# Sixty-four loads of query and key rows issued from the scalar engine's queue in place of the Pool's

## The chip, the cores and the metric

The kernel runs on one core of a Trainium2 chip. A core has a matrix engine (PE, TensorE), a vector engine (DVE), a scalar engine (ACT), a Pool engine (GpSimd) and a sync engine (SP); all of them run their own instruction streams and meet only at semaphores. SP, ACT and Pool can also issue DMA transfers, and the core's 16 DMA engines carry them out. The metric is the device time of one execution in microseconds (us); lower is better.

## The reference, cut to what matters

The layer takes x of shape [2, 1024, 256] in float32. It normalises x and adds two branches to it: causal attention with 16 heads of 16 features and an ALiBi bias, and a mixture of experts (16 experts, the two best for each token, and one shared expert).

```python
xn = _layernorm(x, axis=-1)
x = x + _L0_attn_ref(xn, qkv_w, ...) + _L0_ffn_ref(xn, gate_w, ...)

# attention
qkv = hidden_states @ qkv_w.T + qkv_b
scores = jnp.einsum('bqhd,bkhd->bhqk', q, k) * scale
scores = jnp.where(causal[None, None], scores + bias[None], NEG)
out = jnp.einsum('bhqk,bkhd->bqhd', softmax(scores), v) @ out_w.T + out_b

# experts
_, selected = jax.lax.top_k(sigmoid(x @ gate_w) + expert_bias, 2)
shared = _silu(x @ shared_gate_w) * (x @ shared_up_w) @ shared_down_w
for e in range(16):
    routed += comb[:, e:e+1] * (_silu(x @ gate_e) * (x @ up_e) @ down_e)
```

## The kernel before, in words

The work goes in stages, in this order on every engine.

1. **Projections and routing.** PE forms queries, keys, values and router scores. The queries and keys are cut into three bfloat16 parts each, and SP stores them in DRAM (`qk_parts`, 16 stores, L432). The bias rows of the attention go to DRAM too (`aux_rows`). The router gives every token two slots in a list sorted by expert, and Pool scatters the normalised tokens into it by 32 indirect transfers (`sorted_tokens`, L542).
2. **Shared expert.** Four chunks of 512 tokens. ACT takes one tanh of each (L676), and semaphore `s_g1` tells that PE has made a chunk.
3. **Expert tiles.** The sorted list is 48 tiles of 128 slots. SP loads a tile (`x_in`, L443); PE transposes it (L1137); ACT copies it from PSUM to SBUF (`hx`, L681 for the first three, L691 from then on); PE multiplies it by its expert's weights (L1147); ACT takes a tanh (L686); DVE makes the product (L925, L928); PE multiplies again (L1163); DVE copies the result (L935) and SP stores it (L447). Every tile passes through ACT twice, so nothing of this stage goes on while ACT is elsewhere. Beside the tiles, PE and DVE find the row maxima of attention group 0 (L1176, L942), 32 pieces over the 48 tiles.
4. **Attention.** Eight groups (one sequence, four heads each). Four buffers hold the rows of a group: `qs`/`ks` for groups 0 and 1 (and 4 and 5), `qk` for groups 2 and 3 (and 6 and 7). At its start Pool begins to gather the expert outputs (`yg`, L575). The attention ends with the output projection (L1268).

The helper `load(queue, side, g, half)` fills one half of one side (0 is queries, 1 is keys) of a group's buffer by four transfers: three from `qk_parts` of 3, 2 and 1 parts (L375; 48, 32 and 16 partitions) and one from `aux_rows` (L377; 12 or 15 partitions). It takes the issuing queue as its first argument. A group is four such calls, 16 transfers; groups 0 to 3 are 64 transfers, 16 calls. Below, a call is one set of four transfers. Groups 4 to 7 are another 64, which SP issues during the attention, each group when the buffer it takes is free.

Before, Pool issues groups 0 to 3 behind the scatter. It waits for the shared expert's outputs (`s_sh`), the stores of `aux_rows` and `qk_parts` (`s_auxst`, `s_parts`) and the landed scatter (`s_scat`), the last because group 3's buffer lies where `xn` lay, which the scatter reads. The first use of these loads is the first piece of group 0's maxima, behind expert tile 0 on PE (L1176). Groups 1 to 3 are first used in the attention.

A DMA has a semaphore count that it adds when it lands. Issuing one occupies the issuing engine's stream, and what is behind it in that stream waits.

Of the kernel before, what the change touches and what calls it, by code (L numbers as in the profile page):

```python
# [19 lines left out]
TT = T // P  # L20
KC = D // P
HG = 4
E, F, K_TOP = 16, 128, 2
# [35 lines left out]
NBUF = 4  # L59
RING = 6  # L60
# [79 lines left out]
def build(nc, x, qkv_w, qkv_b, out_w, out_b, slopes, gate_w, ebias, sg_w, su_w, sd_w, e_gu, e_dn,  # L140
          c_ident, c_perm, c_bf, c_pos, c_coef, c_sel, c_row, y):
    ctx = ExitStack()
    with ctx:
# [3 lines left out]
        def sem(name):  # L147
            return ctx.enter_context(nc.semaphore(name))
# [99 lines left out]
        def bank(n, w=CH, m=P):  # L248
            return ps[0:m, n * CH:n * CH + w]
# [33 lines left out]
        s_free = sem("bank_freed")  # L283
        s_res = sem("parts_ready")
        s_mid = sem("mid_ready")
        s_parts = [sem(f"parts_stored{i}") for i in range(RING)]
# [4 lines left out]
        s_auxst = sem("aux_stored")  # L291
# [5 lines left out]
        s_scat = sem("tokens_sorted")  # L297
# [4 lines left out]
        s_sh = sem("shared_out_ready")  # L302
# [49 lines left out]
        NJ, NQK = len(JOBS), len(QKJ)  # L352
# [4 lines left out]
        DMA = 16  # L357
# [5 lines left out]
        def load(queue, side, g, half):  # L363

            dst, order = (q_buf, k_buf)[side][g % NBUF], (Q_PARTS, K_PARTS)[side]
            done = (s_first, s_ld)[g // NBUF][half][g % NBUF]
            cols = slice(half * CH, (half + 1) * CH)
            for t0, n in ((0, 3), (3, 2), (5, 1)):
                p0 = order[t0]
                if side == 0:  # L370
                    src = qkd[0, p0:p0 + 1, g:g + 1, :, :, cols].rearrange("n g d j s -> (g n) d j s")
                    src = src.broadcast_to([n, HD, HG, CH])
                else:
                    src = qkd[1, 0:n, g:g + 1, :, :, cols].rearrange("n g d j s -> (g n) d j s")
                queue.dma_start(dst[HD * t0:HD * (t0 + n), :, cols], src).then_inc(done, DMA)  # L375
            rows = (N_ALIBI, N_AUX)[side]
            queue.dma_start(dst[AUX0:AUX0 + rows, :, cols],  # L377
                         auxd[side, g:g + 1, :, 0:rows, cols].rearrange("g j r s -> r (g j) s")
                         ).then_inc(done, DMA)

        @block.sync
        def _(sp):
# [44 lines left out]
            for i in range(NQK):  # L427
                _, fc, tc = JOBS[QKJ[i]]
                side, g0 = fc // 2, tc // 2 * 4 + fc % 2 * 2
                cols = slice(tc % 2 * CH, (tc % 2 + 1) * CH)  # L430
                sp.wait_ge(s_res, i + 1)
                sp.dma_start(qkd[side, :, g0:g0 + 2, :, :, cols].rearrange("n g d j s -> (g d j) n s"),  # L432
                             parts[:, i % RING, :, :]).then_inc(s_parts[i % RING], DMA)
# [64 lines left out]
        def _(pool):  # L498
# [34 lines left out]
            for n in range(4):  # L533
                side, half = n // 2, n % 2
# [17 lines left out]
            copy_v(0, 0)  # L552
            copy_v(1, 1)

            pool.wait_ge(s_sh, TT // 2)
            pool.wait_ge(s_auxst, 4 * DMA)
            for i, stored in enumerate(s_parts):
                pool.wait_ge(stored, DMA * len(range(i, NQK, RING)))
            pool.wait_ge(s_scat, K_TOP * TT * DMA)
            for g in range(NBUF):  # L560
                for half in range(2):
                    for side in range(2):
                        load(pool, side, g, half)

            for u in range(4):
                pool.wait_ge(s_ys[u], NT // 4 * DMA)
            pool.wait_ge(s_sha, TT // 2)
# [44 lines left out]
        def _(act):  # L612
# [59 lines left out]
            for c in range(4):  # L672
                act.wait_ge(s_g1, c + 1)
                if c >= 2:
                    act.wait_ge(s_h, c - 1)
                sc.activation(th[:, c % 2, :], bank(2 * c), ACT.Tanh, scale=0.5).then_inc(s_th, 1)  # L676

            def evacuate_tokens(k):

                act.wait_ge(s_hxt, k + 1)  # L680
                sc.activation(hx[:, (k + 1) % 2, 1:, :], bank((k + 1) % 2)[:, P:(1 + KC) * P].rearrange(  # L681
                    "p (c n) -> p c n", n=P), ACT.Copy).then_inc(s_hx, 1)
# [645 lines left out]
```

## Time and profile before

| what | us |
|---|---|
| median of 3 runs | 526.53 (524.24 to 529.89) |
| the profiled execution's own time | 525.04 |
| its span, first to last instruction | 523.2 |
| PE busy | 461.9 (88%) |
| DVE busy | 324.3 (62%) |
| ACT busy | 249.4 (48%) |
| POOL busy | 198.4 (38%) |

The profile is of one execution. A wait is charged to the operation that came last. The chain of waits is followed back from the last instruction, at each step to what released it. A queue (SPq, POOLq) is the part of an engine that issues; its rows give the time in which it was issuing a transfer, not the time in which the transfer moved data. For Pool the issuing counts as busy time too; for SP and ACT it doesn't.

### The profile page before, as it was taken

How to read it: one execution, taken by the hardware profiler on the slowest of the kernel's cores; microseconds unless marked ns; L12 is line 12 of the kernel's file. 1: busy time of each engine (PE TensorE's matmuls, PEld its weight loads, DVE VectorE, ACT ScalarE, POOL GpSimd, SP SyncE). 2: the span in 40 equal slices, each digit the busy share in tenths (PEclk: the TensorE clock that was granted, in tenths of full speed). 3: DMA queues.
4: the chain of work that ended last, by engine and by line, in shares of the span. 5: the costliest groups of instructions: out<-in, count | busy, mean ns of one | idle time of the engine just before them, and what ended most of it. 6: DMA issues, size and time to landing. Idle time of an engine off the chain costs nothing.

```text
span 523.2 us, 9031 instructions
## 1 busy us (share of the span) xinstructions
PE 461.9 (88%) x3049; PEld 271.6 (52%) x3050; DVE 324.3 (62%) x610; ACT 249.4 (48%) x567; POOL 198.4 (38%) x239
## 2 busy tenths in 40 slices
PE   4595999737859999995999999999999999999998
PEld 4454788525635666763445354444444444332676
DVE  3869985413425656676867877778586867744232
ACT  2620652112213333332767676676676757678300
POOL 3470777699940000006888888800000000000000
PEclk9799799977779999997999999999999999999999
DMA  9898999799999434424113333221120000010022
GB/s 282 188 403 256 318 323 291 246 170 144 188 174 203 127 110 121 130 79 140 42 49 104 108 86 106 71 76 61 48 82 18 3 3 3 1 13 6 3 89 73
DMA packets 65705, 64.60 MB, mean 123 GB/s; under 512 B 21935, under 2 KB 59539, under 8 KB 65635
## 3 DMA queue, kind: packets, MB, share of 16 engines
q1 hardware_dynamic: 51506, 47.85, 30.9%
q0 software_dynamic: 13056, 15.83, 15.0%
q8 instruction: 24, 0.39, 0.3%
q10 hardware_dynamic: 1104, 0.41, 0.3%
q14 instruction: 15, 0.11, 0.1%
HBM read 37.27 MB, written 27.13 MB: 123 GB/s over the span
## 4 chain that ended last, share of the span: by engine, by line
PE 66%; DVE 13%; DMA 12%; issue 2%; ACT 2%; POOL 2%; SPq 1%; POOLq 0%; DVEq 0%
PE ps L1248 12%; PE ps L1222 10%; PE ps L1234 10%; PE ps L1147 7%; PE ps L1268 5%; DMA x_in<-sorted_tokens 5%; DVE mx L970 5%; PE ps L1043 4%; PE ps L1163 4%; DMA ks<-aux_rows 2%; PE ps L1237 2%; PE ps L1223 2%; PE ps L1137 2%; ACT pt L718 2%; DMA x_sb<-x 1%
## 5 line engine op out<-in xcount | busy, mean ns | idle before, releaser
L718 ACT ACTIVATE pt<-ps 128x512 f32<-128x512 f32 (+3 forms) x384 | 167.1, 494 | 79.7 <-PE ps L1237 55.2
L970 DVE TENSOR_REDUCE mx<-ps 128x1 f32<-128x384 f32 (+6 forms) x189 | 153.3, 863 | 52.4 <-PE ps L1223 51.1
L1248 PE MATMUL ps<-pt,vg 128*32 128x512 f32 (+3 forms) x768 | 71.9, 492 | 0.0
L575 POOL DMA_INDIRECT yg<-sorted_outputs,slot_i x32 | 32.0, 1000 | 94.2 <-DMA sorted_outputs<-y_out 85.4
L1147 PE MATMUL ps<-w_gu,hx 128*128 x192 | 58.3, 432 | 3.8 <-issue 2.2
L1234 PE MATMUL ps<-qs,ks 111*128 111x512 bf16 (+3 forms) x192 | 55.7, 331 | 3.7 <-DMA qs<-nr 3.0
L1234 PE MATMUL ps<-qk 111*128 111x512 bf16 (+3 forms) x192 | 54.9, 329 | 1.8 <-ACT pt L718 0.3
L935 DVE COPY y_out<-ps 128x256 f32<-128x256 f32 x48 | 20.4, 425 | 56.4 <-PE ps L1163 52.7
L1237 PE MATMUL ps<-cbf 128*128 128x128 bf16 x256 | 52.4, 221 | 0.0
L691 ACT ACTIVATE hx<-ps 128x384 f32<-128x384 f32 (+1 forms) x48 | 22.9, 477 | 61.3 <-PE ps L1137 58.6
L1222 PE MATMUL ps<-qk 108*128 108x512 bf16 (+3 forms) x192 | 50.2, 328 | 1.8 <-DVE mx L970 1.3
L1223 PE MATMUL ps<-cbf 128*128 128x128 bf16 x224 | 46.9, 222 | 0.0
L1147 PEld LDWEIGHTS ps<-w_gu,hx 128*128 128x128 f32 x192 | 36.1, 208 | 13.2 <-issue 8.3
L542 POOL DMA_INDIRECT sorted_tokens<-xn,slot_i x32 | 32.8, 1024 | 25.0 <-DVE slot_i L877 15.6
L1222 PE MATMUL ps<-ks,qs 108*128 108x512 bf16 (+3 forms) x144 | 38.5, 335 | 2.4 <-DVE mx L970 1.2
L547 POOL COPY vg<-v_sb 128x512 f32<-128x512 f32 x8 | 4.8, 614 | 89.6 <-PE ps L1248 89.6
L1248 PEld LDWEIGHTS ps<-pt,vg 128*32 128x32 f32 x768 | 19.6, 109 | 33.8 <-issue 20.8
L1163 PE MATMUL ps<-w_dn,hx 128*128 x96 | 33.6, 433 | 1.2 <-ACT hx L691 0.9
L590 POOL TENSOR_SCALAR yg<-yg,gates 128x256 f32<-128x256 f32 x32 | 30.2, 944 | 1.2
L1137 PE MATMUL ps<-ident,x_in 128*128 128x128 f32 x96 | 20.0, 292 | 12.0 <-DMA x_in<-sorted_tokens 11.9
L1234 PEld LDWEIGHTS ps<-qk 111*128 111x128 bf16 x192 | 17.7, 98 | 23.9 <-ACT pt L718 8.4
L686 ACT ACTIVATE te_h<-ps 128x128 f32<-128x128 f32 x48 | 13.3, 277 | 34.5 <-PE ps L1147 34.5
(175 smaller groups left out, 737.9 us busy)
## 6 DMA issues: line engine op xcount, KB each, us to landing
sorted_tokens<-y_out SPq DMA_DIRECT2D x12, 512.0 KB, 5.0
qk_parts<-parts SPq DMA_DIRECT2D x16, 384.0 KB, 3.5
x_in<-sorted_tokens SPq DMA_DIRECT2D x48, 128.0 KB, 2.7
sorted_outputs<-y_out SPq DMA_DIRECT2D x48, 128.0 KB, 1.7
w_gu<-e_gu SPq DMA_DIRECT2D x1, 2816.0 KB, 12.9
x_sb<-x SPq DMA_DIRECT2D x4, 512.0 KB, 8.4
w_dn<-e_dn SPq DMA_DIRECT2D x1, 2048.0 KB, 8.7
y<-x_sb SPq DMA_DIRECT2D x16, 128.0 KB, 1.7
```

The lines of the kernel that those rows point to most:

```text
L542: g_.indirect_dma_start(out=xsd, out_offset=bass.IndirectOffsetOnAxis(ap=slot_i[:, k, t:t + 1], axis=0), in_=xn[:, t, :], in_offset=None). ...
L575: g_.indirect_dma_start(out=yg[:, n % 4, :], out_offset=None, in_=ysd, in_offset=bass.IndirectOffsetOnAxis(ap=slot_i[:, k, t:t + 1], axis= ...
L718: sc.activation(pt[:, s % 4, j, lo:CH], bank(n % 3)[:, lo:CH], ACT.Exp).then_inc(s_exp, 1)
L970: last = v.reduce_max(dst, src, axis=AX.X)
L1137: ins = te.transpose(ps[:, v * CH + (1 + c) * P:v * CH + (2 + c) * P], x_in[:, u, c * P:(c + 1) * P], ident[:, :])
L1147: ins = te.matmul(bank(2 + w, 2 * F), hx[:, 1 - w, 1 + c, :], w_gu[:, bass.ds(e, 1), c, :].rearrange("p o f -> p (o f)"), start=c == 0, st ...
L1163: te.matmul(bank(4 + w, D), hx[:, w, 0, :], w_dn[:, bass.ds(e, 1), :].rearrange("p o f -> p (o f)"), start=True, stop=True).then_inc(s_dn, 1)
L1222: te.matmul(ps[:, at + c:at + e], q, k_buf[g % NBUF][0:K_MAX, j, c:e], start=True, stop=e < w)
L1223: ins = te.matmul(ps[:, at + w - P:at + w], idb, mask_q, start=False, stop=True)
L1234: ins = te.matmul(out[:, lo:CH], k_buf[g % NBUF][0:K_EXP, j, kb * P:(kb + 1) * P], q_buf[g % NBUF][0:K_EXP, j, qc * CH + lo:(qc + 1) * CH] ...
L1237: ins = te.matmul(out[:, lo:lo + P], idb, mask_k, start=False, stop=True)
L1248: ins = te.matmul(ps[32 * j:32 * j + 32, OUT_BANK * CH + lo:(OUT_BANK + 1) * CH], vg[:, par, kb, j, :], pt[:, s % 4, j, lo:CH], start=kb = ...
```

## The change

The wait block and the 16 calls of `load` for groups 0 to 3 leave Pool's stream. ACT's stream gets them, between the fourth tanh of the shared expert and the first copy of an expert tile. ACT waits for `s_free` at its last count (the projections are out of PSUM), `s_auxst` and `s_parts` before the first call, and for `s_scat` only before group 3. The wait on the shared expert's outputs is gone; ACT's own four tanhs already waited for the four `s_g1` counts.

```diff
@@ gpsimd
             copy_v(0, 0)
             copy_v(1, 1)
 
-            pool.wait_ge(s_sh, TT // 2)
-            pool.wait_ge(s_auxst, 4 * DMA)
-            for i, stored in enumerate(s_parts):
-                pool.wait_ge(stored, DMA * len(range(i, NQK, RING)))
-            pool.wait_ge(s_scat, K_TOP * TT * DMA)
-            for g in range(NBUF):
-                for half in range(2):
-                    for side in range(2):
-                        load(pool, side, g, half)
-
             for u in range(4):
                 pool.wait_ge(s_ys[u], NT // 4 * DMA)
             pool.wait_ge(s_sha, TT // 2)
@@ scalar
                 sc.activation(th[:, c % 2, :], bank(2 * c), ACT.Tanh, scale=0.5).then_inc(s_th, 1)
+
+            act.wait_ge(s_free, NJ)
+            act.wait_ge(s_auxst, 4 * DMA)
+            for i, stored in enumerate(s_parts):
+                act.wait_ge(stored, DMA * len(range(i, NQK, RING)))
+            for g in range(NBUF):
+                if g == NBUF - 1:
+                    act.wait_ge(s_scat, K_TOP * TT * DMA)
+                for half in range(2):
+                    for side in range(2):
+                        load(act, side, g, half)
 
             def evacuate_tokens(k):
```

ACT's stream before, from the last tanhs of the shared expert to the first copies of expert tiles (`th` is the shared expert's tanh, `hx` a transposed tile, `te_h` a tile's tanh):

```order
L676 ACTIVATE th<-ps 128x512 [waits shared_h_ready,shared_hidden_ready] x2
L681 ACTIVATE hx<-ps 128x256 [waits tile_transposed] x2
L686 ACTIVATE te_h<-ps 128x128 [waits tile_gate_up_ready] x2
L681 ACTIVATE hx<-ps 128x256 [waits tile_transposed]
L702 UNCONDITIONAL_BRANCH
```

The same place in the changed kernel (its lines from there on are numbered differently):

```order
L666 ACTIVATE th<-ps 128x512 [waits shared_h_ready,shared_hidden_ready] x2
L375 DMA qs<-qk_parts 48x4x512 [waits parts_stored2,parts_stored3,parts_stored1,parts_stored4,parts_stored0,parts_stored5,aux_stored,bank_freed]
L375 DMA qs<-qk_parts 32x4x512
L375 DMA qs<-qk_parts 16x4x512
L377 DMA qs<-aux_rows 12x4x512
L375 DMA ks<-qk_parts 48x4x512
...
L377 DMA qk<-aux_rows 15x4x512
L682 ACTIVATE hx<-ps 128x256 [waits tile_transposed] x2
L687 ACTIVATE te_h<-ps 128x128 [waits tile_gate_up_ready] x2
```

All 64 transfers now stand ahead of the first tile's copy in the same stream.

Pool's stream in the changed kernel, from the scatter to the gather of expert outputs:

```order
L542 DMA sorted_tokens<-xn,slot_i 6144x256 x31
L547 COPY vg<-v_sb 128x32x16 [waits bank_freed]
L547 COPY vg<-v_sb 128x32x16
L565 DMA yg<-sorted_outputs,slot_i 128x256 [waits tile_out_stored3,tile_out_stored2,shared_added,tile_out_stored1,tile_out_stored0]
```

Pool has nothing between its two copies of values and the gather, which waits for all tile outputs as before. SP's stream is the same in both kernels.

## Rows read from the trace of the kernel before

**Rows 1.** The page: busy time by engine, and the chain of waits.
```profile
PE 461.9 (88%) x3049; PEld 271.6 (52%) x3050; DVE 324.3 (62%) x610; ACT 249.4 (48%) x567; POOL 198.4 (38%) x239
...
PE 66%; DVE 13%; DMA 12%; issue 2%; ACT 2%; POOL 2%; SPq 1%; POOLq 0%; DVEq 0%
```

**Rows 2.** Chain of waits, 70 to 160 us: start us, us, what.
```profile
93.02 5.44 DMA sorted_tokens<-xn,slot_i
...
105.11 11.95 DMA ks<-aux_rows
...
118.34 12.69 DMA x_in<-sorted_tokens
...
138.94 15.02 DMA x_in<-sorted_tokens
```

**Rows 3.** Timeline of ACT: start us, duration us, line, operation [idle before].
```profile
94.31 0.60 ACT L676 ACTIVATE th<-ps 128x512 f32<-128x512 f32 x1 [3.91 <-PE ps L1043]
101.03 0.87 ACT L681 ACTIVATE hx<-ps 128x256 f32<-128x256 f32 x2 [6.12 <-PE ps L1137]
...
107.47 0.49 ACT L691 ACTIVATE hx<-ps 128x384 f32<-128x384 f32 x1 [0.64 <-PE ps L1137]
...
158.39 0.49 ACT L691 ACTIVATE hx<-ps 128x384 f32<-128x384 f32 x1 [1.27 <-PE ps L1137]
...
186.45 0.49 ACT L691 ACTIVATE hx<-ps 128x384 f32<-128x384 f32 x1 [1.10 <-PE ps L1137]
...
212.94 0.49 ACT L691 ACTIVATE hx<-ps 128x384 f32<-128x384 f32 x1 [1.13 <-PE ps L1137]
...
233.93 0.28 ACT L691 ACTIVATE hx<-ps 128x128 f32<-128x128 f32 x1 [0.98 <-PE ps L1155]
```

**Rows 4.** Timeline of Pool's queue: its first calls of load and its last.
```profile
99.22 2.75 POOL L375 DMA_DIRECT2D qs<-qk_parts  x3 [4.07 <-DMA sorted_tokens<-xn,slot_i]
101.97 0.56 POOL L377 DMA_DIRECT2D qs<-aux_rows  x1
102.52 2.60 POOL L375 DMA_DIRECT2D ks<-qk_parts  x3
105.11 0.56 POOL L377 DMA_DIRECT2D ks<-aux_rows  x1
...
152.19 0.56 POOL L377 DMA_DIRECT2D qk<-aux_rows  x1
```

**Rows 5.** Waits of PE, 95 to 240 us: total us, times, longest.
```profile
PE ps L1137 <- DMA x_in<-sorted_tokens: 11.9, 5, 3.6
PE ps L1176 <- DMA ks<-aux_rows: 7.9, 1, 7.9
```

**Rows 6.** Timeline of SP's queue: the 16 transfers of group 5, then of group 7.
```profile
306.25 2.46 SPq L375 DMA_DIRECT2D qs<-qk_parts  x3
308.76 0.55 SPq L377 DMA_DIRECT2D qs<-aux_rows  x1
309.35 7.29 SPq L375 DMA_DIRECT2D ks<-qk_parts  x3
...
330.84 0.59 SPq L377 DMA_DIRECT2D ks<-aux_rows  x1
...
369.40 2.27 SPq L375 DMA_DIRECT2D qk<-qk_parts  x3
371.72 0.66 SPq L377 DMA_DIRECT2D qk<-aux_rows  x1
372.42 6.25 SPq L375 DMA_DIRECT2D qk<-qk_parts  x3
378.72 0.59 SPq L377 DMA_DIRECT2D qk<-aux_rows  x1
379.35 5.30 SPq L375 DMA_DIRECT2D qk<-qk_parts  x3
384.69 0.55 SPq L377 DMA_DIRECT2D qk<-aux_rows  x1
385.29 5.26 SPq L375 DMA_DIRECT2D qk<-qk_parts  x3
390.59 0.59 SPq L377 DMA_DIRECT2D qk<-aux_rows  x1
```

**Rows 7.** Source views of L375, L377, L432, L443: issue ns min/median/max; landing.
```profile
L375 SPq DMA_DIRECT2D ks<-qk_parts x12: 737/2806/3348, 277.8 to 327.6; - x12
...
DMA to landing us min/median/max: 5.9/14.1/20.5
...
L432 SPq DMA_DIRECT2D qk_parts<-parts x16: 359/360/366, 55.6 to 81.4; - x16
...
L443 SPq DMA_DIRECT2D x_in<-sorted_tokens x48: 328/345/1242, 98.5 to 221.5; - x48
```

**Rows 8.** Stretches: busy us of PE, PEld, DVE, ACT, POOL; clock, DMA share, GB/s.
```profile
101.00:154.70 53.70, 33.56 (x131) 23.47 (x131) 15.41 (x44) 10.08 (x27) 48.58 (x63) 0.77 1.06 166
...
186.50:213.00 26.50, 26.03 (x130) 17.88 (x131) 16.25 (x46) 9.22 (x25) 0.00 (x0) 1.00 0.39 119
...
379.00:391.00 12.00, 11.76 (x83) 4.75 (x81) 9.97 (x12) 9.21 (x20) 0.00 (x0) 1.00 0.24 77
```

**Rows 9.** Timeline of PE: four matmuls of one tile at low and at full clock.
```profile
117.94 1.99 PE L1147 MATMUL ps<-w_gu,hx 128*128 x4
...
189.24 1.13 PE L1147 MATMUL ps<-w_gu,hx 128*128 x4
```

## The prediction

> **What bounds the kernel now.** I read the page first. PE is busy for 88% of the span and holds 66% of the chain of waits; DMA holds 12% of it and Pool 2% [rows 1]. A share over the whole span doesn't say what a change between 95 and 235 us is worth, so I went to the chain of that stretch. There it isn't PE that sets the end. The chain runs through the scatter's landing, then 11.95 us for a load of group 0's bias rows, then two loads of an expert tile that took 12.69 and 15.02 us [rows 2]. A tile's load usually needs far less. The reader is to see that the loads of groups 0 to 3 stand in the way of the tiles: PE waits 7.9 us for the first of them and 11.9 us for tiles [rows 5].
>
> The timeline of ACT gives the size of that loss, since ACT copies each tile once. Tile 0 is copied at 107.47, tile 12 at 158.39, tile 24 at 186.45 and tile 36 at 212.94 [rows 3]. Between the last two, with Pool silent and the clock at its full level [rows 8], 12 tiles take 26.5 us, 2.21 a tile. The first 12 took 50.9, which is 24.4 more, and the next 12 took 28.1, which is 1.6 more. So at most some **26 us** can be won here, and only if nothing new stands in the way.
>
> **What the change removes.** Pool's queue issued for 53.5 us, from 99.22 to 152.75 [rows 4]. Pool's next work is the gather, which waits for all tile outputs, so its free time is worth nothing. What counts is the 26 us of slow tiles: they vanish if the loads are over before the tiles start. I price this at -26.0.
>
> **What it adds.** ACT ends its fourth tanh at 94.9 and before now copied its first tile at 101.03 [rows 3]. Now 64 transfers stand between these two. The waits ahead of them cost little: the scatter began its last piece at 93.02 and landed 5.44 us later [rows 2], long before group 3 is reached, and the stores of `qk_parts` were issued by 81.8 at the latest [rows 7]. The price is in the issuing.
>
> The trace of before doesn't show ACT issuing these loads, but it shows SP issuing 64 of the same shapes and sizes for groups 4 to 7. The timeline of SP's queue is the view that decides the case. Group 7 takes 21.8 us to issue, from 369.40 to 391.18: its four calls take 3.0, 6.9, 5.9 and 5.9 us [rows 6]. The first call goes out into an empty queue; from the second on, a transfer can be issued only at the pace at which earlier ones move. One large load of keys holds SP for 2.8 us at the median, and the least such hold was 0.74 us [rows 7]. A contiguous load of a tile holds it for 0.35 us and a store of `qk_parts` for 0.36 us [rows 7], so it isn't the number of bytes alone. The share of the 16 DMA engines in use during group 7 was only 0.24 [rows 8]: the queue is full while most of the DMA engines idle.
>
> The Trainium skill has a reason for this. Its page "DMA: Bandwidth & Descriptors", section "Why a DMA increments its semaphore by 16 and not by 1", says that a DMA is split over the largest number of engines, up to 16, that divides the outermost size of both sides, and that on SP's and ACT's queues these are always the lowest-numbered ones, whereas Pool's rotate. By it the loads with 3 and 2 parts outermost would run on three and two engines; the share of 0.24, which is 3.8 of 16, agrees.
>
> ACT issues 16 calls with no pause between groups, so it meets the empty queue once: 3.0 + 6.9 + 14 x 5.9 = 92.5, rounded to **93 us** of issuing. ACT is free at 94.9 + 93 = 188 instead of 101, which puts every tile 87 us later. I take group 7's pace and not group 5's, whose last three calls took 7.36 us each (309.35 to 331.43) [rows 6]: Pool was gathering beside group 5, and nothing moves beside ACT's loads after the first ten microseconds, since tile work stands still.
>
> Ends for this term: below, the pace at which Pool's transfers moved. The last was issued at 152.19 and landed at most 20.5 us later [rows 4, 7], so 16 calls took up to 73.5 us, 4.6 each, and ACT would be free at 168. Above, group 5's pace: 3.1 + 15 x 7.36 = 113.5, and ACT is free at 208.
>
> **A smaller term.** PE will have idled for some 85 us before the tiles. Behind an idle stretch four matmuls of a tile took 1.99 us against 1.13 at full clock [rows 9], the two levels being 1.2 and 2.4 GHz. I add 2 us for two or three tiles at the low level. Between 0 (the slow first 12 tiles that I removed held this already, and my 26.5 for them doesn't) and 6 us (every tile of the first six a microsecond late) is possible. The loads themselves then wait for nobody: group 0 has landed long before its maxima.
>
> **Sum.** 87 - 26 + 2 = +63 us on the last tile, which before was copied at 233.93 [rows 3]. The attention behind it is unchanged, instruction by instruction, and waits for the tiles (maxima of group 0, then the negated maxima), so all of it moves with them. The profiled execution took 525.04 us, 1.84 more than its span; 525.0 + 63 = 588. The median of the runs is 1.5 above that execution, so I forecast **589.5 us**. The likeliest case's own range is 580 to 608.
>
> **The rivals.**
>
> *Faster: issuing costs what SP's other transfers cost.* If ACT could issue without being held, at 0.36 us each [rows 7], 64 would take 23 us, ACT would be free at 118 and the tiles start 17 us late. Most of the 26 us would come back, because group 0 lands early: 17 - 26 + 2 = -7, so 519.5 us. It decides at 0.47 us a transfer, 30 us in all. The Trainium skill's same page, section "Issuing engines are not separate DMA queues", speaks for it: the time to initiate a DMA "is usually small relative to the DMA itself". The trace speaks against it, with 2.8 us for one, and no call of this kind took under 3.0 us even on an empty queue. Chance 0.03 for faster, and 0.02 for ending within 1%.
>
> *ACT's queue holds more than SP's.* If none of ACT's transfers were held, each call would cost what SP's first does, 3.0 us: 16 x 3.0 = 48, free at 143, +42 - 26 + 2 = +18, so 544.5 us. For it speaks only that ACT's queue is nearly unused in this kernel. Against it: SP is held after four or five transfers, so ACT's would have to be some tens deeper. Chance 0.04.
>
> *Pool's pace.* The transfers move at 4.6 us a call as they did from Pool: free at 168, +67 - 26 + 2 = +43, so 569.5 us. SP's rows speak against it, since they show 5.9 with more than three quarters of the DMA engines idle, where Pool's ran beside tile traffic with the share at 1.06 [rows 8]. Chance 0.06.
>
> *The change doesn't do what it says.* The order of ACT's stream shows that it does: no tile's copy stands ahead of a load.
>
> **How the numbers follow.** The likeliest case has 0.85. Range **575 to 608**: it reaches from half-way between Pool's pace and SP's quiet pace up to group 5's pace, and leaves out the first two rivals, most of the third and a slice of the main one. I count a difference under 1% (5 us) as no change, about what a measurement of this kernel can tell. Slower by over 1%: 0.85 + 0.04 + 0.06 = 0.95; within 1%: 0.02; faster: 0.03.
>
> **What would show it.** In the timeline of ACT's queue, L375 and L377 should stand from about 95 to 188 us, each call near 6 us from the third on, with a DMA share near 0.2 to 0.3 once the first 10 us are over. Between some 102 and 188 us PE, DVE and Pool should have no work. ACT's first copy of a tile should be at about 188, the last near 297 (233.93 + 63), and 12 tiles in the first third should take some 27 to 29 us in place of 50.9. The attention should last as long as before. I'd be wrong if the calls took under 4.5 us each or if ACT's tile copies came between them; and the 26 us would be wrong if the first tiles were slow again without the loads beside them.

## The result and the profile after

| | before | changed |
|---|---|---|
| median, us | 525.38 (523.81 to 529.89, 4 runs) | 589.82 (589.38 to 590.48, 4 runs) |
| profiled execution, us | 525.04 | 589.38 |
| its span, us | 523.2 | 587.6 |
| PE busy, us | 461.9 | 453.8 |
| POOL busy, us | 198.4 | 148.0 |

The ratio is 1.1212 (95% interval 1.1138 to 1.1285): the kernel became 64 us slower. The forecast was 589.5 us in a range of 575 to 608.

The page of the changed kernel, busy time and the chain of waits, answers [rows 1]:

```profile
PE 453.8 (77%) x3049; PEld 267.3 (45%) x3050; DVE 323.8 (55%) x610; ACT 249.3 (42%) x567; POOL 148.0 (25%) x175
...
PE 65%; ACTq 16%; DVE 11%; DMA 3%; issue 2%; ACT 2%; SPq 1%; DVEq 0%
```

ACT's queue, which held no part of the chain before, now holds 16% of it, some 94 us. DMA fell from 12% to 3%. ACT's busy time is what it was, since this profile doesn't count issuing in it: whoever reads only busy shares sees an engine at 42% and misses the cause.

Timeline of ACT in the changed kernel, start and duration in us (ACTq is its queue). It answers [rows 3] and has calls as in [rows 6]:

```profile
95.06 0.60 ACT L666 ACTIVATE th<-ps 128x512 f32<-128x512 f32 x1 [3.91 <-PE ps L1044]
95.35 3.69 ACTq L375 DMA_DIRECT2D qs<-qk_parts  x3
99.08 0.58 ACTq L377 DMA_DIRECT2D qs<-aux_rows  x1
99.69 7.61 ACTq L375 DMA_DIRECT2D ks<-qk_parts  x3
107.34 0.60 ACTq L377 DMA_DIRECT2D ks<-aux_rows  x1
107.97 6.15 ACTq L375 DMA_DIRECT2D qs<-qk_parts  x3
...
187.18 5.51 ACTq L375 DMA_DIRECT2D qk<-qk_parts  x3
192.73 0.60 ACTq L377 DMA_DIRECT2D qk<-aux_rows  x1
193.38 0.66 ACT L682 ACTIVATE hx<-ps 128x256 f32<-128x256 f32 x2 [97.72 <-issue]
...
200.04 0.49 ACT L692 ACTIVATE hx<-ps 128x384 f32<-128x384 f32 x1 [0.64 <-PE ps L1138]
...
224.05 0.49 ACT L692 ACTIVATE hx<-ps 128x384 f32<-128x384 f32 x1 [1.14 <-PE ps L1138]
...
250.41 0.49 ACT L692 ACTIVATE hx<-ps 128x384 f32<-128x384 f32 x1 [1.10 <-PE ps L1138]
...
276.83 0.49 ACT L692 ACTIVATE hx<-ps 128x384 f32<-128x384 f32 x1 [1.14 <-PE ps L1138]
...
297.78 0.28 ACT L692 ACTIVATE hx<-ps 128x128 f32<-128x128 f32 x1 [0.98 <-PE ps L1156]
```

The issuing fills 95.35 to 193.33, the whole gap before the first tile's copy. A word on how tiles are counted here and in the prediction: the copy called tile n is the L692 (before: L691) copy of step n of ACT's tile loop. It moves the product of tile n and, up to step 44, the transposed tokens of tile n + 3, which is why it stands some 6.5 us behind the first copy of all; with the tanh, every tile passes through ACT three times. The differences between steps don't depend on the name. The first 12 tiles, steps 0 to 12, now take 24.0 us (200.04 to 224.05) where they took 50.9. Stretches of the changed kernel (us; busy PE, PEld, DVE, ACT, POOL; granted clock, DMA share, GB/s), as [rows 8]:

```profile
107.00:193.00 86.00, 0.00 (x0) 0.00 (x0) 0.00 (x0) 0.00 (x0) 0.00 (x0) 0.50 0.25 77
193.00:200.00 7.00, 4.66 (x13) 3.30 (x13) 1.15 (x4) 1.60 (x5) 0.00 (x0) 0.59 0.17 50
200.00:224.00 24.00, 23.79 (x130) 17.66 (x130) 14.93 (x43) 9.21 (x24) 0.00 (x0) 1.00 0.42 127
```

For 86 us no compute engine does anything, and even then the DMA share is only 0.25, at 77 GB/s. That is the row to learn from: nothing is busy, and yet the queue doesn't go faster. What PE waited for, 90 to 300 us (total, times, longest), against [rows 5]:

```profile
PE ps L1148 <- ACT hx L682: 88.1, 1, 88.1
...
PE ps L1138 <- DMA x_in<-sorted_tokens: 6.3, 1, 6.3
```

The five waits for tiles have become one, the wait for `ks` is gone, and a single wait for ACT replaced them.

### The profile page after: what moved, and what is told of

It reads as the page before. It is cut to its first block, busy times and chain, and to the rows that moved or that the text cites. A ratio compares the mean times of both kernels' runs of the same rounds, so it can differ in the third digit from the quotient of the medians.

```text
span 587.6 us, 9031 instructions
## 1 busy us (share of the span) xinstructions
PE 453.8 (77%) x3049; PEld 267.3 (45%) x3050; DVE 323.8 (55%) x610; ACT 249.3 (42%) x567; POOL 148.0 (25%) x175
## 4 chain that ended last, share of the span: by engine, by line
PE 65%; ACTq 16%; DVE 11%; DMA 3%; issue 2%; ACT 2%; SPq 1%; DVEq 0%
ACTq L375 15%; PE ps L1249 11%; PE ps L1223 9%; PE ps L1235 9%; PE ps L1148 8%; PE ps L1044 6%; PE ps L1269 5%; DVE mx L971 5%; PE ps L1164 4%; PE ps L1238 2%; PE ps L1224 2%; PE ps L1138 2%; ACTq L377 2%; DMA x_sb<-x 1%; PE ps L1177 1%
## 5 line engine op out<-in xcount | busy, mean ns | idle before, releaser
L1148 PE MATMUL ps<-w_gu,hx 128*128 x192 | 54.4, 408 | 89.2 <-ACT hx L682 88.1
L1148 PEld LDWEIGHTS ps<-w_gu,hx 128*128 128x128 f32 x192 | 33.7, 195 | 97.1 <-issue 92.2
L926 DVE SCALAR_TENSOR_TENSOR te_h<-te_h,ps 128x128 f32<-128x128 f32 x48 | 13.3, 278 | 97.7 <-ACT te_h L687 97.7
L692 ACT ACTIVATE hx<-ps 128x384 f32<-128x384 f32 (+1 forms) x48 | 22.9, 477 | 38.8 <-PE ps L1138 36.1
L1164 PE MATMUL ps<-w_dn,hx 128*128 x96 | 32.4, 419 | 1.2 <-ACT hx L692 0.9
L1269 PE MATMUL ps<-wo_t,ot 128*128 128x256 f32 x128 | 28.3, 381 | 1.3 <-DVE ot L1032 1.3
```

The source lines that it names most:

```text
L1148: ins = te.matmul(bank(2 + w, 2 * F), hx[:, 1 - w, 1 + c, :], w_gu[:, bass.ds(e, 1), c, :].rearrange("p o f -> p (o f)"), start=c == 0, st ...
L1164: te.matmul(bank(4 + w, D), hx[:, w, 0, :], w_dn[:, bass.ds(e, 1), :].rearrange("p o f -> p (o f)"), start=True, stop=True).then_inc(s_dn, 1)
L1269: ins = te.matmul(bank(4 + m % 4, D), ot[:, n // QT * 4 + hg, n % QT * P:(n % QT + 1) * P], wo_t[:, hg, :], start=hg == 0, stop=hg == 3)
```

## The experiments

Two theories stood at the start. **Few engines:** a load whose outermost size is 3 or 2 is moved by that many DMA engines, the queue fills, and the issuing engine is held at their pace. **Cost of issuing:** the hold comes with the transfer's bytes, rows or number, or with ACT's queue as such. Ratios below are to the kernel before on the same chip. In the three kernels with "flat" in their names the loads of groups 0 to 3 read other rows than the attention needs, so they show what a load costs and are no kernels to use.

| kernel | median us | ratio, 95% interval |
|---|---|---|
| the changed kernel | 589.82 | 1.121, 1.114 to 1.129 |
| e_act16 | 561.85 | 1.073, 1.068 to 1.078 |
| e_flat48 | 532.17 | 1.013, 1.010 to 1.017 |
| e_half | 570.63 | 1.087, 1.082 to 1.093 |
| e_half_late | 543.77 | 1.036, 1.033 to 1.040 |
| e_pool16 | 500.25 | 0.953, 0.947 to 0.958 |
| e_all16 | 500.37 | 0.953, 0.950 to 0.956 |
| e_paced | 514.54 | 0.980, 0.975 to 0.985 |
| e_pool_flat48 | 514.48 | 0.982, 0.974 to 0.989 |
| e_flat_paced | 522.10 | 0.953, 0.946 to 0.960 |
| e_16_paced | 523.55 | 0.957, 0.948 to 0.965 |

The last two ran on a chip on which the kernel before took 547.32 us; only their ratios compare with the others.

### Loads of one part each, from ACT (e_act16)

```diff
-            for t0, n in ((0, 3), (3, 2), (5, 1)):
+            for t0, n in (... if g >= NBUF else [(t, 1) for t in range(6)]):
...
+                    p0 = order[t0]
-                    src = qkd[1, 0:n, ...]
+                    src = qkd[1, p0:p0 + n, ...]
```

> ACT issues as in the changed kernel, but each load of 3, 2 or 1 parts is cut into loads of one part (16 partitions outermost on both sides): 7 transfers a call in place of 4, 112 in all, same bytes. Theory (a load with 3 or 2 parts outermost runs on so few DMA engines that the queue fills and ACT is held): no hold is left, each transfer costs its bare issue of about 0.6 us, 16 x 7 x 0.6 = 67 us in place of 98, ACT free at about 162 and the time near 558 us (552 to 567). Rival (issuing costs per byte or per row whatever the shape, or the ACT queue is slow in itself): ACT is held for 98 us or longer, with 48 more transfers, so 590 to 617 us.

561.85 us, inside the theory's 552 to 567. Timeline of ACT's queue, third call:

```profile
103.84 3.80 ACTq L377 DMA_DIRECT2D qs<-qk_parts  x6
107.67 0.56 ACTq L379 DMA_DIRECT2D qs<-aux_rows  x1
```

A call went from 6.1 to 4.4 us although it has seven transfers and not four. Each takes 0.63 us (3.80 / 6), from the first call to the last, and ACT was free at 166.0. More transfers of the same rows and bytes cost less time, so the hold wasn't the price of a transfer, of a byte or of ACT's queue as such.

### The same 64 transfers with another outermost size (e_flat48)

```diff
+                if g < NBUF:
+                    src = qkd[side, 0, g:g + n, :, :, cols].rearrange("g d j s -> (g d) j s")
                 queue.dma_start(dst[HD * t0:HD * (t0 + n), :, cols], src).then_inc(done, DMA)
```

> The changed kernel with the same 64 transfers from ACT, of the same sizes and the same 48, 32 and 16 partitions, but the L375 loads of groups 0 to 3 read 48, 32 or 16 neighbouring rows of DRAM, so that the outermost size is 48, 32 or 16 on both sides and not 3, 2 or 1 on the source's. (The rows are not those that the group needs: the scores of groups 0 to 3 are of other values.) Theory (the outermost size decides how many DMA engines move a load, and so how long ACT is held): no hold, 64 x 0.6 = 38 us plus a little at the start, ACT free at about 135 and the time near 530 us (526 to 538). Rival (ACT is held by the bytes or rows of a transfer, or by a queue that is full at a fixed number of transfers): ACT is held for about 98 us again, 585 to 592.

532.17 us. This is the cleanest of the tests, since number, bytes and partitions are those of the change. What it changes beside the outermost size is which rows are read: other ones, and each once, where a load of queries read one part two or three times. e_act16 covers that, since it read the rows of the change and wasn't held either. ACT's queue, the third call and the first copy of a tile; then the stretch of the loads:

```profile
101.69 1.89 ACTq L377 DMA_DIRECT2D qs<-qk_parts  x3
103.62 0.56 ACTq L379 DMA_DIRECT2D qs<-aux_rows  x1
...
136.96 0.66 ACT L684 ACTIVATE hx<-ps 128x256 f32<-128x256 f32 x2 [40.38 <-issue]
```

```profile
98.00:136.00 38.00, 3.34 (x12) 2.01 (x12) 3.60 (x7) 0.00 (x0) 0.00 (x0) 0.58 1.11 213
```

A call took 2.5 us, not 6.1, and the DMA share rose from 0.25 to 1.11. With e_act16 beside it, the bytes, the rows and the number of transfers are ruled out as the cause of the hold: the outermost size is. Behind this measurement stands the Trainium skill, "DMA: Bandwidth & Descriptors", section "Why a DMA increments its semaphore by 16 and not by 1", by whose rule the loads ran on 3 or 2 engines and now on 16. Which engines moved a load isn't in these rows; the share agrees with the number.

The packets of ACT's queue come closer to it (packets, MB, share of 16 engines; the changed kernel at 107 to 193 us, then this one at 98 to 136):

```profile
q10 hardware_dynamic: 6652, 6.32, 23.7%
```

```profile
q10 hardware_dynamic: 7419, 6.67, 95.2%
```

Counted from the same records, two or three packets of ACT's queue were in flight for 73% of the 86 us, and 13 or more for 3%; in this run 13 or more were in flight for 80% of the time. A packet of the changed kernel took 49 ns on average (0.237 x 16 x 86 us / 6652), nearly all of them moving 1 KB. An estimate from that: if three engines share the load of 192 KB and two the load of 128 KB, each moves 64 KB of either, and an engine that is in both moves 128 packets a call, 6.3 us; a call took 6.1.

And 532 is still slower than before: 40 us of bare issuing on ACT put the first copy of a tile 35.9 us later (136.96 against 101.03), more than the 29 us that quiet tiles give back.

### Half of the calls from ACT (e_half, e_half_late)

Against the changed kernel, and condensed:

```diff
-            for g in range(NBUF):
+            for g in range(2):
                 ... load(act, side, g, half)
+            for g in range(2, NBUF):        # in Pool's stream, behind the scatter
+                ... load(pool, side, g, half)
```

> ACT issues groups 0 and 1 only (32 transfers, 8 calls), Pool issues groups 2 and 3 behind the scatter as before. Theory (every microsecond of issuing on ACT moves the tiles by as much): the eighth call ended at 145.0 in the changed kernel, 48 us earlier than the sixteenth, so about 541 us, up to 550 where Pool's transfers slow ACT's. Rival (the price is one fixed thing, such as tiles waiting for the last group to land, not the number of calls): 575 us or more.

570.63 us: the theory's 541 to 550 was missed by 20 us and more, and the rival's 575 wasn't reached. ACT's queue showed why:

```profile
96.16 3.67 ACTq L375 DMA_DIRECT2D qs<-qk_parts  x3
99.87 0.58 ACTq L377 DMA_DIRECT2D qs<-aux_rows  x1
100.48 18.42 ACTq L375 DMA_DIRECT2D ks<-qk_parts  x3
```

Pool issued its own loads of the same shape from 101.58 to 131.36. ACT's second to fourth calls took 19, 17 and 13 us, and the last four, without Pool's, 5.9 to 6.4. Stretches with Pool's loads and without them:

```profile
101.00:131.00 30.00, 1.35 (x4) 0.58 (x4) 0.50 (x1) 0.00 (x0) 24.91 (x32) 0.55 0.95 146
150.00:174.00 24.00, 0.00 (x0) 0.00 (x0) 0.00 (x0) 0.00 (x0) 0.00 (x0) 0.50 0.23 74
```

Together the two queues and the rest moved 146 GB/s. ACT was free at 174.6. I had allowed 9 us for Pool's neighbourhood and it cost 30. So the next run kept Pool away:

```diff
+                        pool.wait_ge(s_yo, 4 + 4 * (4 * (g - 2) + 2 * half + side))
                         load(pool, side, g, half)
```

> ACT issues groups 0 and 1; Pool issues groups 2 and 3, but each of its 8 calls waits until 4, 8, 12 ... 32 tiles are out, so that none runs beside ACT's. Theory (the 29 us by which e_half missed came from Pool's transfers slowing ACT's; alone, ACT's price goes by the number of calls): the eighth call ends near 145 us, the tiles start 48 us earlier than in the changed kernel, and Pool's calls beside the tiles cost 0 to 6 us: 541 to 548 us. Rival (half the calls cost more than half for another reason): 560 or more.

543.77 us.

```profile
144.62 0.66 ACT L691 ACTIVATE hx<-ps 128x256 f32<-128x256 f32 x2 [49.94 <-issue]
```

ACT was free at 144.6, 48.8 us earlier than in the changed kernel, and the time fell by 46.1. The price of the change therefore goes by the calls that ACT issues. And Pool's loads slowed ACT's more than the bytes tell: the 146 GB/s of e_half are well under the 239 of e_pool16 below. Whether ACT's loads slowed Pool's as much isn't shown by these rows.

### Pool again, with even loads (e_pool16, e_all16)

These are the kernel before with the edit of e_act16, for groups 0 to 3 and for all eight.

> The kernel before, Pool issuing, with the loads of groups 0 to 3 cut into one part each (7 transfers a call). If Pool's transfers slow the tiles by uneven use of the DMA engines, as the queue of SP and ACT does, the first 12 tiles take under 40 us in place of 50.9 and the time falls to 510 to 518. If it is the bytes alone that stand before the tile loads, no change: 520 to 530; Pool's issuing lengthens from 50 to about 61 us.

500.25 us, 24 us faster than before and 10 us below the 510 to 518 expected. Stretch of 110 to 140 us, in e_pool16 and then in the kernel before:

```profile
110.00:140.00 30.00, 29.58 (x147) 21.49 (x148) 17.33 (x48) 10.68 (x28) 30.00 (x60) 0.94 0.90 239
```

```profile
110.00:140.00 30.00, 19.19 (x78) 14.51 (x78) 8.27 (x25) 5.37 (x14) 30.00 (x39) 0.72 1.07 170
```

PE is busy for 29.6 of 30 us where it was for 19.2, and DMA moved 239 GB/s at a lower share. The loads of groups 2 and 3 landed sooner too (KB each, median us from issue to landing, first in the kernel before, then in e_pool16):

```profile
qk<-qk_parts POOLq DMA_DIRECT2D x8, 192.0 KB, 16.5
```

```profile
qk<-qk_parts POOLq DMA_DIRECT2D x48, 64.0 KB, 3.2
```

The first 12 tiles took 25.8 us. So the slow tiles came from the way these loads are cut: the kernel before paid for it through the tiles' loads, the changed kernel through ACT's stream. Two things differ here, though, the outermost size and the size of a transfer (at most 64 KB in place of 192); the last runs take them apart.

> The kernel before, Pool issuing groups 0 to 3, with all eight groups' loads cut into one part each (SP's for groups 4 to 7 too). The theory says that SP is held less (28 transfers x 0.6 = 17 us a group in place of 22 to 25). SP's hold was not on the path, so the same time as with Pool's loads cut alone, 498 to 502 us; a gain of up to 3 us if the negated maxima waited behind the loads, a loss if more transfers crowd the queue.

500.37 us, the same. SP was held less (group 7 took 18.4 us in place of 22.5 in e_pool16), and nobody had waited for that hold.

### Is it the shape alone? (e_paced, e_pool_flat48, e_flat_paced, e_16_paced)

```diff
 # e_paced: behind group 0, one call for three tiles; for two tiles in e_flat_paced and e_16_paced
+                        if g:
+                            pool.wait_ge(s_yo, PACE0 + PACE * (4 * (g - 1) + 2 * half + side))
                         load(pool, side, g, half)
```

> The kernel before, Pool issuing, with group 0 at once and each of the other 12 calls held until 4, 7, 10 ... 37 tiles are out (a wait of Pool on the count of copied tile outputs). Theory (the 26 us of slow tiles come from loads that crowd the tile loads): only group 0's four calls crowd them, about half of the loss returns, 508 to 517 us. Rival (the loss is the clock or the first tiles' own): 522 to 530.

514.54 us: 10 us of the 26 came back, with every load cut as it was before, so at least that part of the slow tiles was due to the loads beside them, and not to the clock or the first tiles as such. The first 12 tiles took 36.5 us; PE waited 7.8 us for group 0's loads among them. Each of the next two dozens took 28.1 and 28.3 us in place of 26.4, so even one confined call for three tiles costs something.

> The kernel before, Pool issuing its 64 transfers, but the L375 loads of groups 0 to 3 read 48, 32 or 16 neighbouring rows, so that the outermost size is 48, 32 or 16 on both sides. (Other rows than the group needs: the scores of groups 0 to 3 are of other values.) Theory (the slow tiles of before come from loads that run on 3 or 2 DMA engines, not from the number of transfers or their bytes): the first 12 tiles take 25 to 28 us and the time is 498 to 505 us. Rival (cutting the loads helped because each was smaller, or because 112 transfers leave gaps for the tiles' loads): 518 to 527 us.

514.48 us: neither theory's number. The outermost sizes were even (48, 32 and 16), yet the first 12 tiles took 39.8 us. The chain of waits, 90 to 160 us:

```profile
117.05 10.27 DMA x_in<-sorted_tokens
127.36 0.45 PE ps L1139 x2
127.98 15.90 DMA x_in<-sorted_tokens
```

```profile
110.00:140.00 30.00, 22.87 (x98) 15.90 (x97) 11.35 (x33) 6.92 (x18) 26.70 (x49) 0.87 1.06 239
```

Pool issued a call in 2.2 us (e_pool16: 3.6), 35 us in all, with a share of 1.06 and tile loads of 10 and 16 us on the chain. My reading was that Pool put its bytes before the tiles' loads faster than DMA could move both, so that even loads aren't enough and their pace counts too. The size of a transfer was the other explanation, so:

> Pool's 64 transfers from 48, 32 and 16 neighbouring rows again (other values for groups 0 to 3), but after group 0 each of the other 12 calls waits until 1, 3, 5 ... 23 tiles are out, one call for two tiles (about 4.4 us) where the run before issued one in 2.2 us with the share of the DMA engines at 1.06. Theory (with the loads spread over the engines, what slowed the tiles there was the pace at which Pool put bytes before them): the slow stretch shrinks to group 0's, the first 12 tiles take 26 to 30 us and the time is 499 to 505 us. Rival (the tiles wait because each of Pool's transfers is large, up to 192 KB, whatever the pace): 510 to 516.

A ratio of 0.953, by estimate 500 us on a chip like the first ones (0.953 x 525), with the transfers as large as before.

```profile
131.88 0.49 ACT L696 ACTIVATE hx<-ps 128x384 f32<-128x384 f32 x1 [0.64 <-PE ps L1142]
...
156.34 0.49 ACT L696 ACTIVATE hx<-ps 128x384 f32<-128x384 f32 x1 [1.14 <-PE ps L1142]
```

The first 12 tiles took 24.5 us. Size by itself is ruled out; pace it was. Group 0's four calls weren't paced here nor in e_paced, yet the first 12 tiles took 24.5 us here and 36.5 there, beside confined loads that were paced more slowly. What remains open is that this run and the next were on another chip than the runs they are set against.

> The kernel before with the loads of groups 0 to 3 cut into one part each and the 12 calls behind group 0 held until 1, 3, 5 ... 23 tiles are out. With even loads at Pool's own pace of 3.6 us a call the tiles already ran at their undisturbed rate, so nothing is left to win: 498 to 503 us. If the remaining waits for tiles (2.9 us) go, 1 to 2 us less.

A ratio of 0.957, by the same estimate 502 us, with 27.4 us for the first 12 tiles: nothing was left to win beyond e_pool16.

## Why the prediction was right, point by point

- **ACT is held by the issuing: right, 5 us too small.** 93 us forecast, 98.0 measured. The steady call was 5.9 and came out at 6.1 (14 calls from 107.97 to 193.36). The first two were 3.0 and 6.9 and came out at 4.3 and 8.3: the late expert weights and the first tiles' loads were still moving (159 GB/s from 98 to 107 us against 77 afterwards), a likely cause that no run took apart. These two make 2.7 us of the excess, and the 0.2 us on each of the other 14 the rest. I had said that nothing moves beside ACT's loads after ten microseconds and then priced those ten as if they were quiet too. The first copy of a tile came 92.4 us late instead of 87.
- **Slow tiles go away: right, 2.6 us too small.** The first 12 tiles gave back 26.9 us (50.9 to 24.0) and the next 12 gave 1.7: 28.6 in place of 26, and 24.0 lies below the 27 to 29 that I had named as the sign. My undisturbed rate, 2.21 us a tile, was that of tiles 24 to 36. The undisturbed first 12 run at 2.00 here, and the last 11 at 1.9 in both kernels. In PE's and DVE's code the first and the last 12 tiles are written out and the two dozen between are a hardware loop; that this is the reason was not tested, and the last three copies are also smaller.
- **A slow start of PE: not seen.** I had added 2 us and 0.2 came. The clock stood at 0.50 of full in the 86 idle microseconds and at 0.59 in 193 to 200, but the start from the first copy to tile 0 took 6.66 us against 6.44 before, and from 200 on the clock was full. The kernel before started its tiles no faster, with a clock of 0.74 in 101 to 107.5.
- **The attention moves as a whole: right.** Behind the last tile's copy there are 289.3 us before and 289.8 now.
- **Sum.** 92.4 + 0.2 - 28.6 - 0.1 + 0.5 = 64.4 us of span, against a forecast of 63. One error of 5.4 us upward (ACT) and two downward (2.6 of the tiles, 1.8 of PE's start) nearly cancel in this. The last step was lucky too: I added 1.5 us for the median above the profiled execution, and it was 0.4 (589.82 against 589.38). The mechanism is shown by the runs; the closeness to 0.3 us is luck.
- **Slips in the working.** Half-way between Pool's pace (569.5) and SP's quiet pace (589.5) is 579.5; the lower bound of 575 is a quarter of the way. The upper one, 608, leaves out the 1.5 us that the forecast has: 525 + 83 + 1.5 = 609.5. The 2.8 us that I gave to a large load of keys is the median over all twelve transfers of keys, of 192, 128 and 64 KB; which of them had the 0.74 us isn't in that row.
- **The rivals.** ACT at 0.36 us a transfer is refuted; with no hold at all a transfer took 0.63 us (e_flat48, e_act16), and in e_flat48 the change still lost 7 us. A deeper queue on ACT is refuted by its own rows: the second call was held. Pool's pace of 4.6 us a call is refuted too.
- **What I had not seen.** I read the 12.7 and 15 us of the tiles' loads as the weight of bytes. The share of 1.06 at 166 GB/s [rows 8] could have told me more: the same DMA engines moved 239 GB/s in e_pool16 at 0.90.

## What to carry to other kernels

Before loads are moved to another queue, find the same loads on another queue in the trace and read how long they hold the issuer (here SP's told ACT's within 5 us of 98); an engine that is held in issuing is as blocked as by a wait, and in this profile its busy time doesn't show it. Read the DMA share beside it: a held queue at a share of 0.25 was here the sign that the shape of the loads confined them. Cutting the loads of 3 and 2 parts into loads of 16 rows was worth more (24 us from Pool's queue, by a few lines of `load` and the counts that wait for it) than any choice of the queue. Then watch the pace: even loads issued every 2.2 us slowed the tiles; every 4.4 us, or in smaller pieces every 3.6 us, they didn't.

## What the runs showed of the hardware that I had not expected

- Loads of the confined shape on ACT's and Pool's queues at once held ACT for up to 19 us a call, three times the 6 us that it took alone, while all DMA together moved 146 GB/s.
- DMA share and GB/s part ways: 1.07 at 170 GB/s with loads of 3 and 2 parts, 0.90 at 239 GB/s with loads of one part. A share near 1 isn't a proof that the bytes are the limit. It adds up the times of packets, and these differ: a packet of ACT's queue took 49 ns in the changed kernel and 78 ns in e_flat48 (0.952 x 16 x 38 us / 7419).
- Six loads of 64 KB took Pool about 3.0 us to issue, three of 192, 128 and 64 KB of the confined shape 2.6, and the same three with even outermost sizes 1.65: the shape changes Pool's issuing cost too.
- On one chip the kernel before took 547 us where it took 525 on the others, and the paced kernels' tiles started some 20 us later there. Why is open; it is why ratios are compared.
